# Feed-forward rows transposed by DMA and VectorE instead of TensorE in a fused attention and feed-forward kernel

## What is computed

```python
def attention(X):                       # X is layernorm(x)
    Q = xpos(X @ W_Q); K = xpos(X @ W_K, downscale=True); V = X @ W_V
    p = softmax(einsum('bqd,bkd->bqk', Q, K), axis=-1)
    return einsum('bqk,bkv->bqv', p * 0.9 ** abs(n - m), V)

def fp4_quant_dequant(x):               # in blocks of 16 along the last dim
    scale = maximum(max(abs(xb)) / 6, 1e-12)
    return nearest_of_grid(xb / scale) * scale     # 0, .5, 1, 1.5, 2, 3, 4, 6

def feed_forward(x):                    # x is layernorm(x)
    xq = quant(x)
    h = silu(xq @ quant(w_gate).T) * (xq @ quant(w_up).T)
    return quant(h) @ quant(w_down).T

x = x + attention(layernorm(x))
x = x + feed_forward(layernorm(x))
```

## Time and profile before

| | |
|---|---|
| median of 3 runs | 2549.34 us (2548.3 to 2551.74) |
| profiled execution: span from the first to the last instruction | 2546.6 us |
| mean granted TensorE clock | 0.999 |
| busy share: TensorE, VectorE, GpSimd, ScalarE | 99%, 84%, 71%, 59% |
| share of DMA queue q1 | 24.1% of 16 engines' span |
| one sequence of the loop | 275.62 us |

### The profile page before, as it was taken

The page is one execution under the profiler, slowest core; times in us unless marked ns, Lnnn a source line. Parts: engine busy times, 40 slices in busy tenths (PEclk is TensorE's granted clock), DMA queues, the critical chain, the costliest instruction groups (busy, mean ns, idle before and its releaser), DMA issues.

```text
span 2546.6 us, 51904 instructions
## 1 busy us (share of the span) xinstructions
PE 2518.4 (99%) x16160; PEld 2290.0 (90%) x16160; DVE 2140.9 (84%) x4759; ACT 1489.8 (59%) x2966; POOL 1816.8 (71%) x1929
## 2 busy tenths in 40 slices
PE   8999999999999999999999999999999999999997
PEld 7888879999999999999999999999999999999996
DVE  8999878888878888888888888888888888888886
ACT  5766565656555655566565656565556655555654
POOL 6999956667767676667766776677666776677665
PEclk9999999999999999999999999999999999999999
DMA  8878511122111311131112111131113111211110
GB/s 285 302 271 299 186 50 30 34 86 66 38 40 45 107 37 42 34 106 42 42 34 91 62 38 40 45 107 39 42 34 106 41 42 34 95 58 38 40 38 22
DMA packets 163473, 203.27 MB, mean 80 GB/s; under 512 B 15184, under 2 KB 116752, under 8 KB 163216
## 3 DMA queue, kind: packets, MB, share of 16 engines
q1 hardware_dynamic: 163216, 200.01, 24.1%
HBM read 103.42 MB, written 77.59 MB: 71 GB/s over the span
## 4 chain that ended last, share of the span: by engine, by line
PE 85%; POOL 0%; DVE 0%; issue 0%; ACT 0%; POOLq 0%
PE score L516 27%; PE acc L655 19%; PE ring L516 19%; PE acc L516 9%; PE ring L622 6%; PE ring L675 3%; PE acc L697 1%; PE ring L613 1%; DVE hT L1226 0%; POOL probs L998 0%; ACT probs L823 0%; ACT hT L793 0%; POOL h_buf L1019 0%; POOL xv L1004 0%; POOL h_buf L1013 0%
## 5 line engine op out<-in xcount | busy, mean ns | idle before, releaser
L516 PE MATMUL score<-keys,q_st 128*128 128x512 f32 x3072 | 733.7, 394 | 3.0 <-ACT probs L823 2.6
L516 PEld LDWEIGHTS score<-keys,q_st 128*128 128x128 f32 x3072 | 567.0, 188 | 117.8 <-issue 3.0
L998 POOL TENSOR_TENSOR probs<-probs,decay 128x512 f32<-128x512 f32 (+3 forms) x416 | 450.7, 1097 | 197.5 <-ACT probs L823 197.5
L655 PE MATMUL acc<-vals,pT 128*128 128x256 f32 x3984 | 554.6, 286 | 0.8 <-DVE pT L1226 0.8
L516 PE MATMUL ring<-w_gu,xqT 128*128 128x512 f32 (+1 forms) x2304 | 509.1, 374 | 0.0
L655 PEld LDWEIGHTS acc<-vals,pT 128*128 128x128 f32 x3984 | 498.1, 189 | 7.3 <-DVE pT L1226 2.0
L516 PEld LDWEIGHTS ring<-w_gu,xqT 128*128 128x128 f32 x2304 | 419.0, 188 | 63.6 <-DVE xqT L1226 0.4
L793 ACT ACTIVATE xqT<-ring 128x256 fp32r<-128x256 f32 x128 | 49.3, 385 | 706.9 <-PE ring L613 706.9
L1239 DVE TENSOR_REDUCE smax<-score 128x1 f32<-128x1024 f32 x256 | 312.8, 1222 | 95.6 <-PE score L516 94.1
L1226 DVE TENSOR_TENSOR pT<-ring,pT 128x512 fp32r<-128x512 f32 (+3 forms) x432 | 248.7, 600 | 66.7 <-ACT pT L793 65.5
L1004 POOL TENSOR_TENSOR xv<-xv,xe 128x256 f32<-128x256 f32 x128 | 94.4, 737 | 269.1 <-DVE xv L1079 269.1
(11 more groups left out here) (133 smaller groups left out, 4470.0 us busy)
## 6 DMA issues: line engine op xcount, KB each, us to landing
k_dram<-keys SPq DMA_DIRECT2D x56, 512.0 KB, 4.5
keys<-k_dram SPq DMA_DIRECT2D x56, 512.0 KB, 7.3
edge<-vals SPq DMA_DIRECT2D x288, 64.0 KB, 2.1
q_raw<-q_dram SPq DMA_DIRECT2D x129, 128.0 KB, 2.6
x_in<-X SPq DMA_DIRECT2D x32, 512.0 KB, 4.5
q_dram<-q_stage SPq DMA_DIRECT2D x32, 512.0 KB, 5.4
x_res<-X SPq DMA_DIRECT2D x128, 128.0 KB, 2.1
out<-x_res SPq DMA_DIRECT2D x128, 128.0 KB, 1.7
```

What stands on the lines that cost most here:

```text
L516: mm = pe.matmul(dst, stat(a, k), mov(m, k), start=i == 0, stop=ends and i == n - 1)
L655: mm = pe.matmul(pv_out, pT[g % 2][:, a, j * P:(j + 1) * P], edge[places[m]][:] if kb in edges else vals[m][:, kb, :], start=i == 0, stop= ...
L998: op = pool.tensor_tensor(probs[:, k0:k1], probs[:, k0:k1], decay[:, off + k0:off + k1], ALU.mult)
```

## The change

TensorE no longer transposes hq. GpSimd writes hq in another order of columns, in three instructions instead of two. SP writes the 128x768 block of a tile to DRAM (h_dram), waits until it has landed, and reads it back with four transfers into h_moved, so that 32x32 blocks stand in the quadrant of partitions where they belong. VectorE then turns the blocks with its own 32x32 transpose, two instructions per tile (512 and 256 elements per partition), straight into the banks of the ring. To fit this, the rows of w_gate and w_up are put in another order on the host.

rows_moved stands in SP's step s for tile s-4, behind the keys and the queries and ahead of values, edge rows, store and x rows. The turns stand in VectorE's step t+5, in places that depend on the number of groups. Beside this the third probability group is transposed and split ahead of xqT, and the splits of hT move: with three groups the first half is split by ScalarE ahead of the exponentials and by VectorE ahead of h_levels, with four groups behind them; the second half is split behind them always. The semaphore filled no longer counts hT.

```diff
+MOVED, QUAD = 4, 32
...
+def feed_forward_order():
+    whole = [list(range(k * P + c * QUAD, k * P + (c + 1) * QUAD)) for c in range(CT) for k in range(HK) if k * P + c * QUAD < F]
+    return [f for part in whole for f in part]
 def plan_slots():
...
+            if g + 2 < len(gs):
+                take("pT", s - 1, g + 2)
...
-            if g + 2 < len(gs):
-                take("pT", s - 1, g + 2)
...
 def build(nc, X, WQ, WK, WV, WG, WU, WD, rot_tab, decay_tab, eye, out):
...
+    NF0, NF = (sum(key[0] != "hT" for key in plan) for plan in (first_plan, loop_plan))
...
+        h_dram = nc.dram_tensor("h_dram", (2, P, CT, HK * QUAD), F32, kind="Internal").ap()
...
+        h_moved = [sb(f"h_moved{i}", [P, CT, HK * QUAD]) for i in range(2)]
...
+        sp_passed, h_out, h_back, h_turned = sem("sp_passed"), sem("h_out"), [sem(f"h_back{i}") for i in range(2)], sem("h_turned")
...
         def later(j):
-            return j, NS0 + (j - 1) * NS, loop_plan
-        first, last = (0, 0, first_plan), (B - 1, NS0 + (B - 1) * NS, end_plan)
+            return j, NS0 + (j - 1) * NS, loop_plan, NF0 + (j - 1) * NF
+        first, last = (0, 0, first_plan, 0), (B - 1, NS0 + (B - 1) * NS, end_plan, NF0 + (B - 1) * NF)
         def ahead(i, c, n):
...
+        def halves(at, t):
+            return at[0] * (T // 2) + t // 2 + 1
         def nth(at, *key):
...
+        def nth_filled(at, *key):
+            return at[3] + sum(k[0] != "hT" and i < at[2][key] for k, i in at[2].items())
         def bank(at, *key):
...
+            def passed():
+                sp.sem_inc(sp_passed, 1)
+            def rows_moved(j, t):
+                g, i = j * T + t, t % 2
+                sp.wait_ge(hq_ready, g + 1)
+                passed()
+                if t > 1 or not isinstance(j, int) or j:
+                    sp.wait_ge(h_turned, (g - 1) * 2)
+                    passed()
+                sp.dma_start(h_dram[i].rearrange("p c r -> p (c r)"), hq[i]).then_inc(h_out, 16)
+                sp.wait_ge(h_out, (g + 1) * 16)
+                for c in range(CT):
+                    sp.dma_start(h_moved[i][c * QUAD:(c + 1) * QUAD, :, :], h_dram[i, :, c, :].rearrange("(a i) r -> i a r", a=CT)).then_inc(h_back[i], 16)
             def step(j, s, is_first, more):
...
                     load_q(j, s + 2, more)
+                if s >= MOVED or not is_first:
+                    rows_moved(j, s - MOVED)
...
-            for t in range(T - LAG, T):
-                store(B - 1, t)
+            for s in range(T, T + LAG):
+                if s - MOVED < T:
+                    rows_moved(B - 1, s - MOVED)
+                store(B - 1, s - LAG)
...
-            def attend(at, t, meanwhile, later):
+            def attend(at, t, meanwhile):
...
-                    later(0)
-                    later(1)
...
                         mm.then_inc(pv_done, 1)
+                    if g + 2 < len(gs):
+                        group(at, t, g + 2)
...
-                    if g + 2 < len(gs):
-                        group(at, t, g + 2)
-                    for h in range(2):
-                        if g == min(max(len(gs) - LATER, 0) + h, len(gs) - 1):
-                            later(h)
-            def h_transposed(at, t, h):
-                if has(at, t):
-                    for ks in (range(0, CT), range(CT, HK))[h:h + 1]:
-                        if h == 0:
-                            pe.wait_ge(hq_ready, tile(at, t) + 1)
-                        dst = slot(at, "hT", t, h)
-                        for j, k in enumerate(ks):
-                            mm = pe.transpose(dst[:, j * P:(j + 1) * P], hq[t % 2][:, k * P:(k + 1) * P], ident[:])
-                        mm.then_inc(filled, 1)
             def gate_up(at, t):
...
-                attend(at, s - 1, lambda: x_transposed(at, s - 2), lambda h: h_transposed(at, s - LAG, h))
+                attend(at, s - 1, lambda: x_transposed(at, s - 2))
...
             def upper(dst, src, at, *key):
-                act.wait_ge(filled, nth(at, *key) + 1)
+                act.wait_ge(filled, nth_filled(at, *key) + 1)
...
             def weights(at, i):
-                act.wait_ge(filled, nth(at, "w", i) + 1)
+                act.wait_ge(filled, nth_filled(at, "w", i) + 1)
...
-            def h_transposed(at, t):
-                if has(at, t):
-                    for h, n in enumerate((CT, HK - CT)):
-                        upper(hT[0][:, h * CT:h * CT + n, :].rearrange("p k t -> p (k t)"),
-                              bank(at, "hT", t, h)[:, 0:n * P], at, "hT", t, h)
+            def h_transposed(at, t, h):
+                if has(at, t):
+                    for n in (CT, HK - CT)[h:h + 1]:
+                        act.wait_ge(h_turned, 2 * tile(at, t) + h + 1)
+                        act.activation(hT[0][:, h * CT:h * CT + n, :].rearrange("p k t -> p (k t)"), bank(at, "hT", t, h)[:, 0:n * P], ACT.Copy).then_inc(hi_done, 1)
             def exponentials(at, s):
...
-                        act.wait_ge(filled, nth(at, "gu", t, p) + 1)
+                        act.wait_ge(filled, nth_filled(at, "gu", t, p) + 1)
...
                     exponentials(at, s)
...
+                attend(at, s - 1, range(2, min(n, 3)))
                 x_transposed(at, s - 2)
-                attend(at, s - 1, range(2, n - 1))
-                if n > 2:
-                    attend(at, s - 1, range(n - 1, n))
-                h_transposed(at, s - LAG)
+                attend(at, s - 1, range(3, n))
+                if n <= 3:
+                    h_transposed(at, s - LAG, 0)
...
                     exponentials(at, s)
+                if n > 3:
+                    h_transposed(at, s - LAG, 0)
+                h_transposed(at, s - LAG, 1)
...
-                        pool.wait_ge(filled, nth(at, "xqT", t - 1) + 1)
+                        pool.wait_ge(filled, nth_filled(at, "xqT", t - 1) + 1)
...
-                        pool.wait_ge(filled, nth(at, "hT", t - 2, 1) + 1)
+                        pool.wait_ge(h_out, (g - 1) * 16)
...
-                    n = HALF // QB
-                    last, scale = (x[:, -n:].unsqueeze(1).to_broadcast([P, 2, n, QB]) for x in (blocks(hv[t % 2]), spread(hs[t % 2][:], HB)))
-                    pool.tensor_tensor(hq[t % 2][:, F - HALF:FT].rearrange("p (a b k) -> p a b k", a=2, k=QB), last, scale, ALU.mult)
-                    pool.tensor_tensor(blocks(hq[t % 2][:, 0:F - HALF]), blocks(hv[t % 2][:, 0:F - HALF]), spread(hs[t % 2][:, 0:HB - n], HB - n), ALU.mult).then_inc(hq_ready, 1)
+                    v, q, b = hv[t % 2], hq[t % 2], hs[t % 2]
+                    front = FT // 2
+                    def parts(ap, width):
+                        return ap.rearrange("p (c r) -> p c r", r=width)
+                    def fine(ap):
+                        return ap.rearrange("p c (b k) -> p c b k", k=QB)
+                    def repeated(ap):
+                        return ap.unsqueeze(3).to_broadcast([P, 2, ap.shape[2], QB])
+                    wide, narrow = HK * QUAD, (HK - 1) * QUAD
+                    pool.tensor_tensor(fine(parts(q[:, front:], wide)[:, :, narrow:]), fine(parts(v[:, 0:front], wide)[:, :, narrow:]),
+                                       repeated(parts(b[:, 0:front // QB], wide // QB)[:, :, narrow // QB:]), ALU.mult)
+                    pool.tensor_tensor(fine(parts(q[:, front:], wide)[:, :, 0:narrow]), fine(parts(v[:, front:], narrow)),
+                                       repeated(parts(b[:, front // QB:], narrow // QB)), ALU.mult)
+                    pool.tensor_tensor(blocks(q[:, 0:front]), blocks(v[:, 0:front]), spread(b[:, 0:front // QB], front // QB), ALU.mult).then_inc(hq_ready, 1)
             def step(at, s):
...
+            def h_turned_blocks(at, t, place):
+                for h in range(2):
+                    if has(at, t) and place == turn_place(at, t, h):
+                        dve.wait_ge(h_back[t % 2], halves(at, t) * CT * 16)
+                        dve.wait_ge(freed, nth(at, "hT", t, h) - (RING - 1) + PRIME)
+                        k0, k1 = (0, CT) if h == 0 else (CT, HK)
+                        dve.transpose(bank(at, "hT", t, h)[:, 0:(k1 - k0) * P].rearrange("p (k a j) -> p k a j", a=CT, j=QUAD),
+                                      h_moved[t % 2][:, :, k0 * QUAD:k1 * QUAD].rearrange("p a (k i) -> p k a i", i=QUAD)).then_inc(h_turned, 1)
+            def turn_place(at, t, h):
+                n = len(groups((t + LAG - 1) % T))
+                return ("begun", "x") [h] if n <= 3 else ("x", "all")[h]
             def residual(at, t):
...
                 attend(at, s - 1, range(min(n, 2)))
+                h_turned_blocks(at, s - LAG, "begun")
                 maxima(at, s, 1)
...
+                attend(at, s - 1, range(2, min(n, 3)))
                 x_transposed(at, s - 2)
-                attend(at, s - 1, range(2, n))
-                for h in range(2):
-                    h_transposed(at, s - LAG, h)
```

(13 more changed lines are left out.)

## The result

The changed kernel takes 2589.49 us (median of 4 runs, 2587.4 to 2591.49) against 2549.36 us before (4 runs beside them, 2548.3 to 2551.74): ratio 1.0156, interval 1.0142 to 1.017, so 1.6% slower. The forecast was 2532 us, and the range ended at 2556.

What follows compares the result with a forecast made beforehand. It took TensorE as the bound, busy 99%, so each instruction removed is time won: 81.8 - 8 - 16.8 - 28 - 4.6 - 7.5 = 16.9 us off, from 2549.3 to 2532 us; eight-in-ten range 2496 to 2556.

Steps and rivals of the forecast that it cites:

- transposes removed, less VectorE in short steps: TensorE loses 0.66 us on each of 124 tiles, 81.8 us won; VectorE's excess in short steps takes back 8.
- hT's splits moved: Four-group steps, 48 in all: TensorE waits for hT's first half, split behind the exponentials; 16.8 us lost (0 to 31).
- tail: After the last tile's hq: transfers, GpSimd and a turn before TensorE can go on, plus clock; 7.5 us lost (5 to 11).
- 0.44 + 0.22 = 0.66 us: TensorE time per tile of the six feed-forward transposes (four, then two), read from the chain through one step.
- Turns: VectorE's two 32x32 transposes cost 1.1 us per tile, hidden in most steps; short steps lose 1.0 us a sequence.
- TensorE waits 0.35 us: Four-group steps: gate/up wants the ring bank that hT's first half frees before VectorE's split ends; 0.35 us each.
- there the second half is free at about the time it is wanted: nothing: Three-group steps: splitting hT's second half behind the exponentials costs TensorE nothing.
- 7 x 4.0 = 28 us: Steps loading the next sequence's keys: edge rows queue behind the moved rows on SP; TensorE stands 4.0 us (2 to 7).
- VectorE's own wait for the read-back lies inside: At the key loads, VectorE waits for the moved rows to 1134.5, within TensorE's stop for edge rows, adding nothing.
- 7 x 0.65: Lower TensorE clock after each stop at the key loads, half of 1.3 us counted: 4.6 us lost (0 to 9).
- The second: Rival: four-group steps wait 0.66 us and not 0.35, cancelling the saving; 15 us more, 2547 us; chance 0.12.
- VectorE as the bound: Rival: turns cost 2.2 us per tile, so VectorE limits each sequence; 2580 us, decides from 2.0 us; chance 0.16.

Runs made afterwards that it cites:

- e4: Changed kernel with hT's splits back ahead of the exponentials (ScalarE) and the feed-forward levels (VectorE) in all steps: 2556.75 us.
- e9: e5's kernel, moved rows ahead of the store in the last five steps, and in a sequence's last step their write ahead of the keys' second half: 2529.03 us.
- e8: Kernel before, with only the third probability group transposed and split ahead of xqT, on all engines; nothing moved: 2549.27 us.
- e5: e4's kernel with 24 instead of 34 warm-up transposes, so the loop branch stands 20 TensorE instructions earlier: 2554.39 us.
- e6: e5's kernel; in a sequence's last step SyncE issues v_raw and edge rows ahead of moving the feed-forward rows: 2551.34 us.
- e12: e9's kernel with VectorE making each turn twice, first into a spare SBUF buffer, then into PSUM: 2568.98 us.
- e1: Changed kernel with 128 semaphore increments ahead of TensorE's first warm-up transpose, shifting all its later instructions: 2590.54 us.
- e2: Changed kernel with 236 semaphore increments ahead of TensorE's first warm-up transpose: 2610.49 us.
- e3: Kernel before with only 177 TensorE semaphore increments added at the start, putting its branch where the changed kernel's stands, counted in blocks of 256: 2610.85 us.
- e10: Changed kernel with only ScalarE's splits of hT ahead of the exponentials in all steps; VectorE's stay as changed: 2580.75 us.
- e11: Changed kernel with only VectorE's splits of hT ahead of the feed-forward levels in all steps; ScalarE's stay as changed: 2736.72 us.

## Why the prediction was wrong

The mechanisms in it were mostly the right ones; three sizes and one unseen stop added up to 57 us, the first term alone to 24. The traces' step lengths give the sum anew. Over all steps the changed kernel is 25.7 us longer, e4 4.5 shorter, e9 29.3 shorter. In e9 step 0 still stands 1.3 to 3.1 us over the kernel before, 17.5 in all, where 0.4 under it would be its share (my estimate): without any stop the steps would be 29.3 + 17.5 + 2.8 = 49.6 shorter.

| term | forecast | measured |
|---|---|---|
| transposes removed, less VectorE in short steps | 81.8 - 8 = 73.8 won | 49.6 won |
| hT's splits moved | 16.8 lost | 25.7 + 4.5 = 30.2 lost (e4) |
| boundary: stops and clock | 28 + 4.6 = 32.6 lost | 49.6 - 4.5 = 45.1 lost |
| tail | 7.5 lost | 71.3 - 58.0 = 13.3 lost |
| sum | 16.9 won | 39.0 lost; the span 39.3, as the start is 0.2 later |

**Transposes removed: the step that failed most is "0.44 + 0.22 = 0.66 us".** The pieces of the chain are counted from end to end, and matmuls overlap. The timeline of the kernel before has the same step from start to start:

```profile
1013.33 0.60 PE L675 MATMUL ring<-ident,hq_buf 128*128 128x128 f32 x4
1013.68 1.66 PE L655 MATMUL acc<-vals,pT 128*128 128x256 f32 x12
1015.18 0.38 PE L675 MATMUL ring<-ident,hq_buf 128*128 128x128 f32 x2
1015.32 1.28 PE L655 MATMUL acc<-vals,pT 128*128 128x256 f32 x9
```

0.35 + 0.14 = 0.49 us. Steps with three groups gain about that (0.5 to 0.6 in all kernels without other stops). Steps with four gain 0.3, which is some 15 of the 24 us that this term lacks: the 21 products between take 2.62 us here and 2.81 in e4, where weight loads wait up to 0.2 us for a probability split of VectorE that had the transposes as its cover. That the cover is the reason is argued and not tried; e8 shows only that the new order by itself isn't.

**Turns.** Right in size (1.17 for 1.1). The cost in short steps, forecast 1.0 a sequence, is lower: with early splits and no stop, steps 1 and 2 are 0.06 and 0.4 under the kernel before, where 0.5 each was to be had. The changed kernel's loss in step 2 belongs to the splits.

**Splits moved.** "TensorE waits 0.35 us" in four-group steps is near what was measured: in steps 7 to 11 gate/up's three blocks together take 4.06 us from start to start instead of 3.80, 0.26 more. Wrong was "there the second half is free at about the time it is wanted: nothing". In step 2 and at the boundary (step 15) the second half cost 1.6 and 0.6 us, since on VectorE it stands behind the levels. In step 2 these meet GpSimd's multiplications, and in step 6 too, where it is the first half that costs 1.0 us. That meeting wasn't in the forecast at all.

**Boundary.** "7 x 4.0 = 28 us" for the edge rows was right as a mechanism: e5 shows it with 3.7 us, seven times, and the half-clock price behind it. In the changed kernel it stays hidden under a stop that the trace of before could not show, the branch, whose place in the program the removed transposes had moved (335 fewer records up to its first execution). The two overlap; together they cost 45 us and not 33. "VectorE's own wait for the read-back lies inside" was wrong too, as e6 shows: it is the same size, and it appears once the edge rows are early. "7 x 0.65" for the clock was small: in e5 six stops of 2.9 to 4.3 us cost 0.9 to 2.4 us more in their step.

**Tail.** Right kind, half the size: 13.3 for 7.5. Each of the last tiles pays for move and turn again, not the last one only (waits of 5.1, 2.8 and 3.6 us), and clock is lost with it, 0.82 over the stretch.

**Rivals.** None came out as written. The second (splits cancel the saving in four-group steps) described the steps right, by a smaller saving rather than a longer wait, but its 2547 left the boundary and step 2 as they were. VectorE as the bound lies on the right side, and its 2580 is the nearest time, but with the wrong cause: the turns took 1.17 us and not 2.2. That is luck; e12 gives its real price. The chances for same and slower add up to 0.10 and 0.24, not to 0.11 and 0.23.

**Open.** Why the branch is short 20 instructions ahead of its place and not at it is not known; no other places than those of e1, e2 and e5 were tried. How much of the 45 us at the boundary is clock alone is only known as a difference. How much of the moved splits' cost is the order and how much the meeting with GpSimd was not separated.

## What to carry to other kernels

Work taken off a saturated engine pays what it takes from start to start, less the cover that it gave to others' results; look in each kind of step for the next result that now comes last. A transfer that must be waited for does not belong behind megabytes on the same queue: one write moved ahead of half the keys was worth 21 us, while moving the waiters around (e6) was worth 3 at most. And after any change in the number of instructions in a loop, look at the loop's branch in the trace first: here a mere shift made an untouched kernel 40 us, 1.6%, slower by its step lengths.

## What the runs showed of the hardware

A taken loop branch of TensorE cost 0.35 to 0.56 us (before, e1, e2, e5 to e9, e12) or 5.7 to 6.4 us (after, e3, e4, e10; 4.1 to 5.4 in e11), by its place in the program; a long one ended 1.35 to 1.5 us behind the landing of an instruction packet. The scores behind it ran partly at the lower clock (7.1 us for 5.7). Behind waits of 2.9 to 4.3 us the granted clock over 5 us was 0.50 to 0.71 in six cases of seven (e5), behind waits of 0.9 to 2.1 us it was 1.00 (e9). A semaphore increment on TensorE at the start was not free: 128, 177 and 236 of them delayed the attention by 14.2, 21.2 and 30.3 us, 0.11 to 0.13 us each. VectorE's 32x32 turns of 512 and 256 32-bit elements cost about the same into PSUM (722 and 449 ns) as into SBUF (707 and 426, in e12). A pass of VectorE over 704 elements with two tensors as inputs lasted 0.9 us alone and 1.86 us beside two multiplications of GpSimd. A 384 KB write landed in 2.3 us as a rule and 8.4 to 9.4 us behind 4 MB of keys.
